# Last group's low-rank FFN in two halves of queries, with five re-orderings in a causal attention kernel on 8 cores

## What is computed

```python
def _L0_attn_ref(x, Wq, Wk, Wv, Wo):
    q = jnp.einsum('bse,ek->bsk', x, Wq)
    k = jnp.einsum('bse,ek->bsk', x, Wk)
    v = jnp.einsum('bse,ev->bsv', x, Wv)
    scores = jnp.einsum('bqk,bsk->bqs', q, k)
    scores = jnp.where(causal_mask[None], -jnp.inf, scores)
    attn = jax.nn.softmax(scores * Wq.shape[1] ** (-0.5), axis=-1)
    out = jnp.einsum('bqs,bsv->bqv', attn, v)
    return jnp.einsum('bqv,vo->bqo', out, Wo)
def _L0_ffn_ref(x, U1, V1, b1, U2, V2, b2):
    P = jnp.einsum('bsd,dr->bsr', x, U1)
    H = jax.nn.gelu(jnp.einsum('bsr,rf->bsf', P, V1) + b1)
    Q = jnp.einsum('bsf,fr->bsr', H, U2)
    return jnp.einsum('bsr,rd->bsd', Q, V2) + b2
x = _layernorm(x + _L0_attn_ref(x, Wq, Wk, Wv, Wo), axis=-1)
x = _layernorm(x + _L0_ffn_ref(x, U1, V1, b1, U2, V2, b2), axis=-1)
```

## Time and profile before

| | us |
|---|---|
| median of 3 runs | 1909.01 |
| lowest and highest run | 1626.38, 1943.98 |
| profiled execution, device time | 1627.65 |
| its span, slowest core (core 0) | 1626.1 |
| spans of the other cores | 1620.1 to 1625.2 |
| PE, DVE, ACT, POOL busy on core 0 | 1558.3, 695.7, 608.8, 91.2 |

### The profile page before, as it was taken

One profiled execution on the slowest core, in us unless ns is written; L12 is line 12 of the kernel. 1 busy time (PEld: TensorE's weight loads), 2 busy tenths in 40 slices (PEclk: granted clock), 3 DMA queues, 4 the chain that ended last, 5 costly groups with the idle time before them and its releaser, 6 DMA issues.

```text
span 1626.1 us, 26313 instructions; the slowest of 8 cores (1620.1 to 1626.1 us)
## 1 busy us (share of the span) xinstructions
PE 1558.3 (96%) x8507; PEld 777.4 (48%) x8672; DVE 695.7 (43%) x1410; ACT 608.8 (37%) x1237; POOL 91.2 (6%) x137
## 2 busy tenths in 40 slices
PE   6899999999999999999999999999999999999985
PEld 2445455454545454454544544544544544464442
DVE  2437356435444354442545324436330643633063
ACT  3633633540564044620446400546410344640023
POOL 0012010001000100000000010000010000001000
PEclk9999999999999999999999999999999999999998
DMA  9899696665465613739146565346457244215401
GB/s 284 257 268 175 147 117 216 153 123 195 156 142 114 211 63 132 117 118 297 64 150 113 103 212 190 104 155 130 92 184 255 105 154 146 77 53 183 154 0 52
DMA packets 72047, 242.48 MB, mean 149 GB/s; under 512 B 4960, under 2 KB 10224, under 8 KB 61296
## 3 DMA queue, kind: packets, MB, share of 16 engines
q1 hardware_dynamic: 60320, 190.86, 35.8%
q0 software_dynamic: 11600, 49.93, 18.9%
HBM read 252.40 MB, written 52.43 MB: 187 GB/s over the span
## 4 chain that ended last, share of the span: by engine, by line
PE 94%; issue 2%; ACT 1%; DMA 1%; DVE 1%; DVEq 0%; SPq 0%; ACTq 0%
PE ps L674 28%; PE ps L642 28%; PE ps L727 7%; PE ps L626 7%; PE ps L814 7%; PE ps L719 7%; PE ps L658 4%; PE ps L616 2%; PE ps L742 2%; PE ps L767 2%; PE ps L604 1%; PE ps L833 1%; DMA wf<-wkt 1%; PE ps L689 0%; ACT zt L874 0%
## 5 line engine op out<-in xcount | busy, mean ns | idle before, releaser
L674 PE MATMUL ps<-p_sb,x_ring 128*128 128x512 bf16 (+3 forms) x2247 | 462.9, 361 | 6.8 <-ACT ot L848 3.2
L642 PE MATMUL ps<-x_ring,zt 128*128 128x512 bf16 (+2 forms) x2164 | 444.9, 362 | 4.7 <-ACT zt L848 2.7
L674 PEld LDWEIGHTS ps<-p_sb,x_ring 128*128 128x128 bf16 x2304 | 217.5, 98 | 229.8 <-issue 4.9
L642 PEld LDWEIGHTS ps<-x_ring,zt 128*128 128x128 bf16 x2208 | 210.7, 98 | 230.6 <-issue 3.8
L982 DVE TENSOR_REDUCE nm<-ps 128x1 f32<-128x512 f32 (+3 forms) x288 | 185.7, 647 | 297.6 <-PE ps L642 287.8
L858 ACT ACTIVATE p_sb<-ps,nm 128x512 bf16<-128x512 f32 (+3 forms) x288 | 187.5, 651 | 252.4 <-DVE nm L982 252.1
L874 ACT ACTIVATE zt<-ps,b_sb 128x512 bf16<-128x512 f32 x256 | 169.4, 691 | 39.8 <-PE ps L719 38.3
L727 PE MATMUL ps<-zt,wf 128*128 128x512 bf16 x502 | 145.0, 379 | 4.6 <-ACT zt L874 4.1
L719 PE MATMUL ps<-p_sb,wf 128*128 128x512 bf16 x500 | 144.8, 379 | 1.5 <-DVE p_sb L1069 0.9
L1125 DVE CAST ot<-ps 128x512 bf16<-128x512 f32 x32 | 22.1, 692 | 268.0 <-PE ps L674 268.0
L848 ACT ACTIVATE ot<-ps 128x512 bf16<-128x512 f32 x32 | 19.1, 597 | 287.9 <-PE ps L674 287.9
(11 more groups left out here) (82 smaller groups left out, 962.2 us busy)
## 6 DMA issues: line engine op xcount, KB each, us to landing
x_ring<-xtb SPq DMA_DIRECT2D x67, 1024.0 KB, 6.0
x_ring<-xnb SPq DMA_DIRECT2D x48, 1024.0 KB, 6.5
xnb<-xn POOLq DMA_DIRECT2D x8, 2048.0 KB, 37.3
x<-xo SPq DMA_DIRECT2D x24, 512.0 KB, 7.9
xtb<-xt POOLq DMA_DIRECT2D x12, 1024.0 KB, 25.5
out<-x POOLq DMA_DIRECT2D x24, 512.0 KB, 7.4
x_ring<-xnb SPq DMA_DIRECT2D x16, 768.0 KB, 4.9
wf<-wvt SPq DMA_DIRECT2D x8, 512.0 KB, 17.4
```

Source lines behind the costliest of these rows:

```text
L642: mm = t.matmul(ps[b][:, 0:w], zt[:, ec * 512 + j * 128:ec * 512 + (j + 1) * 128], xs[:, off + ec * 512:off + ec * 512 + w], start=(ec == ...
L674: mm = t.matmul(ps[b][:, q0:512], ring[:, off + k * step:off + k * step + 128], P[:, p0 + q0:p0 + 512], start=(c == 0 and k == 0), stop=(c ...
```

## The change

Six edits:

1. `product_by_rows` takes tiles 0 to 3 of the first half of wvo; tiles 4 to 7 remain with `product_by_tiles`. The row pieces' casts are waited for one by one.
2. `blocks_of`: the first chunk of S in each group goes through blocks 3, 2, 1, 0; the others stay. DVE and ACT follow.
3. `early_turns`: block 0 of up to six chunks, min(6, 4g). For group 0 none, for group 1 four as before.
4. In the weighted sum, e = 0 and 1 leave out the last two chunks in the loop with the turns and take them afterwards, each e in one piece.
5. x1's transposes of h = 1 are evicted by DVE in all groups but the last.
6. The last group's FFN runs in two halves of 256 queries (blocks 0, 1 and blocks 2, 3): transposes and p1 of the first, transposes of the second, hidden layer of the first, p1 of the second, output of the first, hidden layer and output of the second. DVE norms the first half's rows before the second half's output.

```diff
+def blocks_of(ti):
+    return (3, 2, 1, 0) if ti == 0 else (0, 1, 2, 3)
...
 def early_turns(g):
-    return [(c, 0) for c in range(4)] if g > 0 else []
+    return [(c, 0) for c in range(min(6, 4 * g))]
...
                     for ec in range(8):
-                        if ti == 0 and j == 0:
+                        if ti == 0 and j == 3:
                             t.wait_ge(out_of["z"], 8 * g + ec + 1)
...
-            for k in range(8):
-                cast_done(t, ("v", k, None))
-            for i in range(4):
-                cast_done(t, ("o", 2 * i, 0))
-            product_by_tiles("w", wvt, wo_sb, 0)
+            product_by_rows("w", wvt, wo_sb, 0, range(4),
+                            lambda k: [("v", k, None)] + [("o", k, 0)] * (k % 2 == 0))
+            product_by_tiles("w", wvt, wo_sb, 0, range(4, 8))
...
                 for c in range(nt):
                     for j in range(4):
                         emptied(("t", g, c, j))
-                    for e in range(2):
-                        values_chunk(g, e, c)
+                    if c < nt - 2:
+                        for e in range(2):
+                            values_chunk(g, e, c)
                     if c + 2 < nt:
                         for _, j in later_turns(g, c + 2):
                             turn_tile(g, c + 2, j)
-                for e in range(2, 8):
-                    for c in range(nt):
+                for e in range(8):
+                    for c in range(nt - 2 if e < 2 else 0, nt):
                         values_chunk(g, e, c)
...
-            for rc in range(2):
-                ffn_in(NG - 1, rc)
-            ffn_hidden(NG - 1)
-            ffn_out(NG - 1)
+            last = NG - 1
+            turn_x1(last, range(2))
+            for rc in range(2):
+                ffn_in(last, rc, (0,))
+            turn_x1(last, range(2, 4))
+            ffn_hidden(last, (0,))
+            for rc in range(2):
+                ffn_in(last, rc, (1,))
+            ffn_out(last, (0,))
+            ffn_hidden(last, (1,))
+            ffn_out(last, (1,))
...
+                for j in range(4 if g < NG - 1 else 0):
+                    tile_full(v, ("xt", g, j, 1))
+                    b = psb[RING[("xt", g, j, 1)] % RB]
+                    v.tensor_copy(x1_turned(j, 1), b[:, 0:512].rearrange("p (n k) -> p n k", k=128)
+                                  ).then_inc(out_of["xt_dve"], 1)
                 if g == NG - 1:
                     for rc in range(2):
-                        ffn_in(g, rc)
+                        ffn_in(g, rc, (0,))
...
-            ffn_middle(NG - 1)
-            ffn_out(NG - 1)
-            for k in range(8):
-                ln2_piece(NG - 1, k)
+            last = NG - 1
+            ffn_middle(last, (0,))
+            for rc in range(2):
+                ffn_in(last, rc, (1,))
+            ffn_out(last, (0,))
+            for k in (0, 1, 4, 5):
+                ln2_piece(last, k)
+            ffn_middle(last, (1,))
+            ffn_out(last, (1,))
+            for k in (2, 3, 6, 7):
+                ln2_piece(last, k)
```

More of the change, by code:

```diff
@@ L75, in scores @@
         for t in ts:
-            for j in range(4):
+            for j in blocks_of(t):
                 put(ring, ring_out, ("s", g, t, j), "exp")
@@ L166, in stream_numbers @@
             number[("s", g, t)] = len(used)
-            used.append(("full", RING[("s", g, t, 3)] + 1))
+            used.append(("full", RING[("s", g, t, blocks_of(t)[-1])] + 1))
         nu = n_units(g)
@@ L370, in turned_to, with queries, x1_turned @@
             return bass.AP(t, at + c * 4096 + h * 2048 + j * 128, [[cols, 128], [512, 4], [1, 128]])
+        def queries(part):
+            return (0, 512) if not part else (256 * part[0], 256)
+        def x1_turned(j, h):
+            return bass.AP(ot, h * 2048 + j * 128, [[4096, 128], [512, 4], [1, 128]])
         def tile_full(eng, key):
@@ L749, in ffn_hidden @@
                 for fc in range(32):
-                    hidden(g, fc)
+                    hidden(g, fc, part)
                     if g == 0 and fc == 4:
@@ L962, in _ @@
                         z_out(g + 1, f)
-            gelus(NG - 1)
+            for part in range(2):
+                gelus(NG - 1, (part,))
         @blk.vector
```

174 lines of the change are left out of this document (98 added, 76 removed).

## The result

| us | before | after |
|---|---|---|
| median | 1767.87 (4 runs) | 1611.3 (4 runs, 1610.35 to 1611.46) |
| ratio after / before, 95% interval | | 0.9905 [0.9888, 0.9922] |
| spans of the 8 cores | 1620.1 to 1626.1 | 1606.0 to 1608.7 |
| PE, DVE, ACT, POOL busy, core 0 | 1558.3, 695.7, 608.8, 91.2 | 1553.5, 706.1, 598.3, 91.5 |

The change makes the kernel 0.95% faster, and the interval of 0.17% to either side excludes "no change". (The median of before is that of disturbed executions, up to 1943.98 us; the ratio, and every median and ratio further on, is of undisturbed ones, here 1626.38 and 1626.72 us.) The forecast was 1612.0 us.

What follows compares the result with a forecast made beforehand. TensorE (PE), busy 96% of the span, was taken as the bound, so only closing its gaps saves time. Terms -6.2 - 4.5 + 3.3 + 3.5 - 3.6 - 8.5 = -16.0 took 1627.65 to 1612 us, range 1601 to 1621.

Steps and rivals of the forecast that it cites:

- F: Last group's FFN in halves: earlier first gelu gains 0.8 us, shorter DVE tail 7.7; -8.5 us in all.
- The class: Verdict: measurement can tell about 2% from no change, 1595 to 1660; faster 0.04, same 0.94, slower 0.02.
- A: First half of WvWo by rows: PE's wait for casts and the half clock behind it go; -6.2 us.
- B: First chunk of S reversed: eight waits for the last z tile's eviction go, 0.56 us each; -4.5 us.
- C: Six early turns in groups 2 to 7: DVE's later cast and evictions stall PE, 0.55 us lost per group; +3.3 us.
- D: Weighted sum's last two chunks: e=2's 0.57 us wait goes, a 1.1 us wait for turn evictions comes; +3.5 us.
- E: x1's transposes evicted by ACT and DVE: third tile ready 0.5 us earlier; -3.6 us over seven groups.
- if the clock falls elsewhere: Listed sign that the forecast is wrong: PE's clock falling at another place; no size given.
- Rival 2: ACT or the clock limits the last group's halves: gelus +2.8 us, longer low clock 1.7; 1614 to 1616; 15%.
- Rival 4: Last group's FFN: weight loads not hidden at 256 columns, 144 loads at 0.09 us; +13, 1625 us; 4%.

Runs made afterwards that it cites:

- tiles: The changed kernel with the first half of WvWo tile by tile again, all else kept: 1615.84 us, ratio 0.9929 to before.
- order0: The changed kernel with the first chunk of S in order 0, 1, 2, 3 again, all else kept: 1616.16 us, ratio 0.9932 to before.
- turns4: The changed kernel with four early turns again instead of six, all else kept: 1607.87 us, ratio 0.9889 to before.
- oldsum: The changed kernel with the weighted sum's old order, all else kept: 1605.67 us, ratio 0.9874 to before.
- xtact: The changed kernel with all of x1's transposes evicted by ACT again, all else kept: 1615.14 us, ratio 0.9924 to before.
- splitonly: The kernel before with only the last group's FFN in halves added: 1618.21 us, ratio 0.9945 to before.
- nosplit: The changed kernel with the last group's FFN in one piece of 512 queries again, all else kept: 1620.43 us, ratio 0.996 to before.
- latep1: The changed kernel with p1 of the last group's first half moved behind all of x1's transposes: 1614.8 us, ratio 0.9928 to before.
- cover4: The changed kernel with four early turns and e=1's matmuls of chunk nt-3 held back until behind the last turns: 1599.04 us, ratio 0.9833 to before.

## Why the prediction was right or wrong, point by point

The sum was right to 0.7 us (1612.0 against 1611.3), and the mechanism of every term but F held. That the total came so close is luck in part. The sum starts from the profiled execution, 1627.65 us, which is 1.1 above the mean of the two runs of before that the ratio uses (1626.38 and 1626.72), and its gain is 1.1 too small (16.0 against 17.1 by S to end); the two cancel. What it said of the verdict was wrong.

**The class.** "What a measurement of this kernel can tell from no change is about 2%" is the step that failed. It came from no row: the runs of before that the ratios use agree within 0.16% (1625.92 to 1628.45), and the ratio has an interval of 0.17% to either side, so the measured 0.95% is a change clear of the scatter. A forecast of 1.0% less was, by that, a forecast of "faster", and its 94% for "no change" contradicted its own sum.

| term | forecast | measured | from |
|---|---|---|---|
| A, WvWo by rows | -6.2 | -5.8 (-3.8 without the clock's fall) | tiles |
| B, first chunk reversed | -4.5 | -5.0 | order0, stages |
| C, six early turns | +3.3 | +3.0 | turns4, stages |
| D, last two chunks | +3.5 | +4.2 | oldsum |
| E, two evicting engines | -3.6 | -3.3 | xtact, stages |
| F, halves | -8.5 | -9.5 to -11.0 | splitonly, nosplit |
| sum | -16.0 | -16.4 to -17.9; S to end -17.1 | |

**A** held as told: no wait, no fall of the clock there, 26.22 us on all cores. The 2.7 us for the clock was high for four cores, on which the fall costs 1.6 to 1.7, and right for three, with 2.7 to 3.0.

**B** held; 0.56 per group was 0.62. Of "hidden, with 1 us to spare" half a microsecond is left, because DVE comes late from E's evictions and norms.

**C** held: the two stalls are where they were put (before the sixth turn and before the first hidden tile). In group 4 they are 0.15 and 0.10 us by core 4's rows, with 0.165 each 0.58; the forecast had 0.55. DVE's cast did begin later, and its evictions follow it at 0.35 us as before.

**D**: the stall is what was forecast, 0.94 + 0.165 = 1.1 us on core 4, and the signal of 0.25 us lies inside the "0.14 to 0.3". What was mis-sized is the wait of e = 2 that the edit closes: 0.57, from the mean of core 0's table (3.2 us over 8, which missing records lengthen), where the row of group 4 itself has 0.29 + 0.165 = 0.46 and the stages 0.47. The net is 0.63 per group and not 0.5. That the longer wait in group 0 can bring the clock down was not foreseen either, though "if the clock falls elsewhere" stood among the signs of being wrong: it did, on core 0.

**E** held: 0.49 per group.

**F** was 1.0 to 2.5 us too small, by a wrong path. The tail was worked out as -7.7 and is -7.3 on core 0 and -7.7 on core 4 with the four pieces as counted. But the last down-projection ends 2.2 us earlier than before on core 0 (53.4 against 55.6 us behind the first wvo matmul) and 2.7 on core 4 (53.6 against 56.3), not 0.8: "PE's clock is 0.50 from 1566.6 to 1573.4; I leave it there" is the second step that failed. It looked at the clock as a property of the place, where latep1 shows that it follows what PE does there. The 1.95 us that this step added are about the difference.

**The rivals.** Rival 2's two halves both fell: gelus of 256 columns follow each other every 0.36 us (1.94 us for five, the last one 0.51), inside PE's 0.436 per hidden tile. Rival 4 fell: in the row of 1580 to 1594 PE has 126 recorded matmuls in 14.00 us and was never idle, which is 0.111 us each with a weight load each, and no more than 0.109 where one or two records are missing; the term had 0.108. The Trainium skill, page "TensorE: Matmul & The Clock Gate", section "Back-to-back issue gap", would have added 7.2 us, an estimate. The trace does not agree with it here: 288 matmuls at 0.111 instead of 0.108 us are 0.9 us at most.

**Not seen before the run**: that C and D could both be had, by another order of the same matmuls (cover4, 11 to 12 us more).
